# Attention output stage: one semaphore per kind of result, the first product two turns ahead of its norm, and the first norm's scale and shift applied in ScalarE's copy

## The reference, cut to what matters

```python
out = outs.transpose(1, 0, 3, 2, 4).reshape(Bb, Ll, dm)
out = _ln(out, post_w, post_b, eps=1e-05)      # first norm, scale post_w, shift post_b
return out @ wo                                # y, 256 wide
```

## Time and profile before

| what | value |
|---|---|
| median of 3 runs | 451.33 us (451.16 to 452.99) |
| the profiled execution's own time | 449.57 us |
| its span, first to last instruction | 447.8 us |
| granted TensorE clock, mean over the span | 0.93 of full |
| busy share of the span | PE 86%, DVE 66%, ACT 63%, POOL 39% |
| the changed stage | 239.6 to 308.5 us, 23 turns |

### The profile page before, as it was taken

How to read it: one execution, slowest core, us unless ns; L and a number is a source line. 1 busy time by engine, 2 the same in 40 slices (tenths; PEclk the granted TensorE clock), 3 DMA queues, 4 the chain that set the end, 5 groups by cost and what they waited for, 6 DMA issues and landing times. The chain is left out here.

```text
span 447.8 us, 11346 instructions
## 1 busy us (share of the span) xinstructions
PE 384.3 (86%) x3744; PEld 262.3 (59%) x3744; DVE 293.7 (66%) x1029; ACT 281.6 (63%) x710; POOL 173.4 (39%) x298
## 2 busy tenths in 40 slices
PE   1999998959999999999982999975698587799993
PEld 1544343438777787778761667762443164577883
DVE  4757529355777777777773487864869975455185
ACT  4778676554766766776663566653679992551634
POOL 1405728023888888888875013233000000000003
PEclk9999999987999999999996799985979977899997
DMA  8221233251122222222235300000000000000003
GB/s 236 34 84 37 73 103 93 86 176 37 51 54 67 70 63 57 68 70 57 61 117 154 72 1 0 2 0 1 0 1 1 0 18 10 1 2 3 4 1 94
DMA packets 33008, 23.07 MB, mean 52 GB/s; under 512 B 10046, under 2 KB 32716, under 8 KB 32972
## 3 DMA queue, kind: packets, MB, share of 16 engines
q1 hardware_dynamic: 31724, 22.54, 18.4%
q10 hardware_dynamic: 1248, 0.07, 0.2%
HBM read 13.13 MB, written 9.47 MB: 50 GB/s over the span
## 5 line engine op out<-in xcount | busy, mean ns | idle before, releaser
L1466 POOL TENSOR_TENSOR win<-win,lng 128x512 f32<-128x512 f32 x2 | 2.5, 1273 | 125.5 <-ACT win L1745 125.5
L967 ACT ACTIVATE win<-bank 128x384 f32<-128x384 f32 (+1 forms) x124 | 44.2, 412 | 9.7 <-PE bank L910 9.1
L479 PE MATMUL bank<-w,hT 128*128 128x385 f32 x128 | 45.4, 495 | 0.4 <-ACT stage L605 0.4
L888 PE MATMUL bank<-win,wst 128*32 128x128 f32 x1024 | 44.2, 283 | 1.3 <-ACT kd L962 1.3
L479 PEld LDWEIGHTS bank<-w,hT 128*128 128x128 f32 x128 | 23.2, 189 | 24.5 <-issue 11.4
L888 PEld LDWEIGHTS bank<-win,wst 128*32 128x32 f32 x1024 | 26.6, 110 | 9.2 <-ACT kd L962 1.5
L1239 ACT ACTIVATE std_<-mv_,cst 128x2 f32<-128x2 f32 (+1 forms) x46 | 13.5, 296 | 28.5 <-DVE mv_ L1217 14.5
L1189 POOL TENSOR_TENSOR xn<-xn,out_b 128x128 f32<-128x128 f32 x16 | 7.3, 455 | 50.9 <-ACT xn1T L1255 50.9
L1034 POOL TENSOR_SCALAR xh<-raw,bmv,brs 128x128 f32<-128x128 f32 x32 | 25.5, 797 | 2.6 <-DVE brs L1086 2.5
L877 PE MATMUL bank<-win,cst 128*128 128x128 f32 x128 | 25.1, 278 | 0.9 <-ACT raw L988 0.9
L1027 POOL TENSOR_TENSOR xkm<-win,wst 128x256 f32<-128x256 f32 x32 | 19.7, 615 | 12.5 <-PE bank L926 6.0
(11 more groups left out here) (300 smaller groups left out, 1117.3 us busy)
## 6 DMA issues: line engine op xcount, KB each, us to landing
rows_scratch<-stage SPq DMA_DIRECT2D x32, 192.5 KB
win<-rows_scratch SPq DMA_DIRECT2D x32, 192.5 KB, 2.4
attn_scratch<-ob SPq DMA_DIRECT2D x32, 64.0 KB
att<-attn_scratch SPq DMA_DIRECT2D x4, 512.0 KB, 4.1
xt<-in_L_attn_x SPq DMA_DIRECT2D x4, 256.0 KB, 4.3
out<-win SPq DMA_DIRECT2D x4, 256.0 KB, 2.4
cst<-in_constants SPq DMA_DIRECT2D x1, 408.0 KB, 5.2
w<-in_L_attn_wk SPq DMA_DIRECT2D x2, 128.0 KB, 4.3
```

The lines of the kernel that those rows point to most:

```text
L479: mm = nc.tensor.matmul(rows_bank(i, h)[:, 0:RC], hT[:, k, i * P:(i + 1) * P], w4[:, k, h, :], start=(k == 0), stop=(k == 1))
L888: mm = nc.tensor.matmul(dst[32 * b:32 * b + 32, 0:F], v[:, at:at + 2 * K], w_sb[:, state, first_slot(b) + h, :], start=False, stop=(h == 1 ...
L967: nc.scalar.activation(w_sb[:, state, at:at + n, :], bank[b][:, 0:n * F].rearrange("f (h g) -> f h g", h=n), ACT.Copy).then_inc(w_done, 1)
```

## The change

The stage keeps its arithmetic but for the first norm. It now runs as follows.

- Each kind of result has a semaphore of its own: `yn_done`, `y2_done`, `y_mm`, `h_mm`, `h_read`, `norm_done`, `x_mm`, `x_done`. `mm_done` and `act_norms` are gone; DVE no longer waits at a turn's start for PE's previous turn.
- y is made in turn 2 and its norm is taken in turn 4 instead of 3 (three banks hold y in rotation), and the steps behind it move with it: transposes of y2 in turn 5, h in 6, its statistics in 7, xn1 in 8, the transposes of xn1 in 9. There are 25 turns.
- One `std` and one reciprocal serve all three norms of a turn. xn1 of a tile is written one turn later than its statistics.
- On PE the transposes of yn and of y2 come first, then h, then y, then the transposes of xn1, which now wait for DVE and ACT at a turn's end and not at its start.
- `wo` is loaded as it is. ACT's copy of the transposed yn becomes two pieces of 128 columns, each with its own scale and shift per partition (`post`), instead of one plain copy of 256 columns. The one-row bias product is gone, and in `layer0_in` the products L551, DVE's copy L420 and DVE's two scalings L424.

The core of the difference; of the lines taken out of the three programs of `layer0_out`, which stand in full in the functions above, the plus lines are the replacement:

```diff
-        wo_bias = take(7 * HD, HD, 1)
+        post = take(7 * HD, 4).rearrange("p (n k) -> p n k", n=2)
...
-                    dve.wait_ge(bias_mm, 2)
-                    ch.mark(nc.vector.tensor_copy(wo_bias, bank[5][0:1, 0:HD]))
...
-                        ch.mark(nc.vector.tensor_scalar(wo[:, k, :], wo_raw[:, k, :], post_w[:, k:k + 1], None, ALU.mult))
...
-                        mm = nc.tensor.matmul(bank[5][0:1, 0:HD], post_b[:, k:k + 1], wo_raw[:, k, :],
-                                              start=(k == 0), stop=(k == 1))
-                    mm.then_inc(bias_mm, 1)
...
+        A_TR, Y_PROD, Y_STAT, H_TR, H_PROD, H_STAT, X_OUT, X_TR = 1, 2, 4, 5, 6, 7, 8, 9
+        TURNS = NT + X_TR
+        NORMS = NT + H_STAT
+        TURN_W = NT + Y_STAT
+        LAST_CP = TURN_W + 1
...
+        y_bank = lambda n: bank[(2, 3, 7)[n % 3]][:, 0:HD]
+        h_bank = lambda n: bank[4 + n % 2][:, 0:D]
+        x_bank = bank[6][:, 0:P]
...
+                for n in range(NORMS + 1):
                     p = n % 2
+                    ks = []
+                    if on(n, 0):
+                        if n % B == 0:
+                            dve.wait_ge(at_in[n // B], 16)
+                        mark(nc.vector.bn_stats(st[:, 0, :], at[:, tile(n), :]))
+                        ks.append(0)
+                    if on(n, Y_STAT):
+                        dve.wait_ge(y_mm, n - Y_STAT + 1)
+                        mark(nc.vector.bn_stats(st[:, 1, :], y_bank(n - Y_STAT)))
+                        ks.append(1)
+                    if on(n, H_STAT):
+                        i = tile(n - H_STAT)
+                        dve.wait_ge(h_mm, n - H_STAT + 1)
+                        nc.vector.tensor_tensor(xt[:, i, :], xt[:, i, :], h_bank(n - H_STAT), ALU.add).then_inc(h_read, 1)
+                        dve.wait_ge(h_read, n - H_STAT + 1)
+                        mark(nc.vector.bn_stats(st[:, 2, :], xt[:, i, :]))
+                        ks.append(2)
+                    if ks:
+                        dve.wait_ge(stats, marks[0])
                         for k in ks:
                             ins = nc.vector.bn_aggr(mv[:, p, k, :], st[:, k, :])
                         ins.then_inc(var_done, 1)
+                    if on(n, X_OUT):
+                        i = tile(n - X_OUT)
+                        dve.wait_ge(rs_done, 2 * n)
+                        nc.vector.tensor_scalar(xn1[:, i, :], xt[:, i, :], mv[:, 1 - p, 2, 0:1], rs[:, 1 - p, 2:3],
                                                 ALU.subtract, ALU.mult).then_inc(norm_done, 1)
+                    if ks:
+                        dve.wait_ge(std_done, n + 1)
+                        nc.vector.reciprocal(rs[:, p, :], std[:, p, :]).then_inc(rs_done, 1)
+                        dve.wait_ge(rs_done, 2 * n + 1)
+                        nc.vector.scalar_tensor_tensor(out=shift[:, p, :], in0=mv[:, p, 0:2, 0], scalar=-1.0, in1=rs[:, p, 0:2],
+                                                       op0=ALU.mult, op1=ALU.mult).then_inc(rs_done, 1)
...
+                    if n < NORMS:
+                        act.wait_ge(var_done, n + 1)
+                        nc.scalar.activation(std[:, p, :], mv[:, p, :, 1], ACT.Sqrt, bias=con("eps5")).then_inc(std_done, 1)
+                    if 0 < n <= LAST_CP:
                         act.wait_ge(tr_mm, n)
+                        if on(n, A_TR):
+                            for k in range(2):
+                                ins = nc.scalar.activation(tT[:, p, 0, k * P:(k + 1) * P], bank[p][:, k * P:(k + 1) * P],
+                                                           ACT.Identity, bias=post[:, 1, k:k + 1], scale=post[:, 0, k:k + 1])
+                        if on(n, H_TR):
                             ins = nc.scalar.activation(tT[:, p, 1, :], bank[p][:, HD:2 * HD], ACT.Copy)
                         ins.then_inc(cp_done, 1)
+                    if on(n, 0) or on(n, Y_STAT):
+                        act.wait_ge(rs_done, 2 * n + 2)
                     if on(n, 0):
                         nc.scalar.activation(yn[:, p, :], at[:, tile(n), :], ACT.Identity, bias=shift[:, p, 0:1],
+                                             scale=rs[:, p, 0:1]).then_inc(yn_done, 1)
+                    if on(n, Y_STAT):
+                        nc.scalar.activation(y2[:, p, :], y_bank(n - Y_STAT), ACT.Identity, bias=shift[:, p, 1:2],
+                                             scale=rs[:, p, 1:2]).then_inc(y2_done, 1)
+                    if on(n, X_TR):
+                        i = tile(n - X_TR)
+                        act.wait_ge(x_mm, n - X_TR + 1)
+                        nc.scalar.activation(xn1T[:, i * P:(i + 1) * P], x_bank, ACT.Copy).then_inc(x_done, 1)
...
+                    if 3 <= n <= LAST_CP:
                         pe.wait_ge(cp_done, n - 2)
+                    if on(n, A_TR):
+                        pe.wait_ge(yn_done, n)
                         for k in range(2):
                             ins = nc.tensor.transpose(bank[p][:, k * P:(k + 1) * P], yn[:, 1 - p, k * P:(k + 1) * P], con("ident"))
+                    if on(n, H_TR):
+                        pe.wait_ge(y2_done, n - H_TR + 1)
                         for k in range(2):
                             ins = nc.tensor.transpose(bank[p][:, HD + k * P:HD + (k + 1) * P], y2[:, 1 - p, k * P:(k + 1) * P], con("ident"))
+                    if n <= LAST_CP:
+                        ins.then_inc(tr_mm, 1)
+                    if on(n, H_PROD):
+                        i = tile(n - H_PROD)
                         pe.wait_ge(cp_done, n - 1)
+                        if n - H_PROD >= 2:
+                            pe.wait_ge(h_read, n - H_PROD - 1)
+                        dst = h_bank(n - H_PROD)
                         nc.tensor.matmul(dst, ffnT[:, i * P:(i + 1) * P], con("ident"), start=True, stop=False)
                         for k in range(2):
                             ins = nc.tensor.matmul(dst, tT[:, 1 - p, 1, k * P:(k + 1) * P], up[:, k, :], start=False, stop=(k == 1))
+                        ins.then_inc(h_mm, 1)
+                    if on(n, Y_PROD):
+                        pe.wait_ge(cp_done, n - 1)
+                        for k in range(2):
+                            ins = nc.tensor.matmul(y_bank(n - Y_PROD), tT[:, 1 - p, 0, k * P:(k + 1) * P], wo[:, k, :],
+                                                   start=(k == 0), stop=(k == 1))
+                        ins.then_inc(y_mm, 1)
+                    if on(n, X_TR):
+                        pe.wait_ge(norm_done, n - X_TR + 1)
+                        wait(pe, x_done, n - X_TR)
+                        nc.tensor.transpose(x_bank, xn1[:, tile(n - X_TR), :], con("ident")).then_inc(x_mm, 1)
```

More of the change, by code:

```diff
@@ L1185, in _ @@
                 pool.wait_ge(m1.w_in, 16 * m1.loads)
-                for n in range(7, TURNS):
-                    i = tile(n - 7)
-                    pool.wait_ge(cp_done, n)
+                for n in range(NT):
+                    i = tile(n)
+                    pool.wait_ge(x_done, n + 1)
                     nc.gpsimd.tensor_tensor(xn1[:, i, :], xn1[:, i, :], m1.out_b[:], ALU.add)
@@ L1216, in _ @@
                         for k in ks:
                             ins = nc.vector.bn_aggr(mv[:, p, k, :], st[:, k, :])
-                        if not ks:
-                            ins = nc.vector.memset(mv[:, p, 2 * part, :], 1.0)
                         ins.then_inc(var_done, 1)
-                    dve.wait_ge(std_done, 2 * n + 1)
-                    nc.vector.reciprocal(rs[:, p, 0:2], std[:, p, 0:2]).then_inc(rs_done, 1)
-                    dve.wait_ge(rs_done, 3 * n + 1)
-                    nc.vector.scalar_tensor_tensor(out=shift[:, p, :], in0=mv[:, p, 0:2, 0], scalar=-1.0, in1=rs[:, p, 0:2],
-                                                   op0=ALU.mult, op1=ALU.mult).then_inc(rs_done, 1)
@@ L1253, in _ @@
[L1253 to L1255 removed]
+                            ins = nc.scalar.activation(m1.w_outT[:].rearrange("p k d -> p (k d)"), bank[3][:, HD:2 * HD], ACT.Copy)
                         ins.then_inc(cp_done, 1)
[L1257 to L1259 removed]
+                    if on(n, 0) or on(n, Y_STAT):
+                        act.wait_ge(rs_done, 2 * n + 2)
```

103 lines of the change are left out of this document (20 added, 83 removed).

## The result

| | before | after |
|---|---|---|
| median of the runs, us | 452.16 (451.16 to 453.87, 4 runs) | 427.73 (424.98 to 431.72, 4 runs) |
| profiled execution, us | 449.57 | 425.5 |
| its span | 447.8 | 423.7 |
| stage (first memset of `mv` to layer 1) | 239.70 to 308.53 = 68.83 | 238.12 to 292.02 = 53.90 |
| layer 1 (same code in both) | 139.3 | 131.7 |

The ratio is 0.944, 95% interval 0.935 to 0.952: faster. Ratios and intervals leave out executions more than 1.5% above the fastest of the same kernel (one of e14's among them, 539.70 us at a mean clock of 0.643); in the batches of e5 to e12 and of e17 and e18 these are most of before's, which puts the ratio there about 0.01 above the quotient of the medians. The direction was right; the size was not. Forecast were 439.9 and a range of 436 to 445.5, a gain of 11.4; the measured gain is 24.4, and 24.1 in the span of the two profiles.

The account below looks back on a forecast made before the run. PE's own work and a two-turn ring were taken to bound the stage at 3.17 us a turn. At 2.6 a turn the stage saves 10.4 and the input stage 1.0, 11.4 together: median 439.9 us, range 436 to 445.5.

Parts of the forecast that it names:

- The ring of 2.55: Stage's middle: ACT's copies, yn, y2 and PE's transposes of y2 form a one-turn ring of 2.55 us.
- rings at 2.41: Stage's middle: DVE's own ring at 2.41 us and PE's work at 2.41 to 2.65 interlock with ACT's ring.
- What bounds the kernel now: Stage before the change: PE's 3.03 us a turn and a two-turn ring of 3.15 to 3.2 each both bound.
- Start: Stage's first turns at clock 0.50: PE bounds at 2.56 us a turn; turn 5 starts at 251.6.
- End: Stage's end from turn 20: before's 8.80 us at clock 0.50 plus 1.0 for the longer pipeline.
- rival 2: Larger gain: turn of 2.55 us and PE at full clock to the stage's end; 437.1 us, chance 0.12.
- The four turns without a new tile: Stage's turns 16 to 20: DVE's ring is 2.07 us without first statistics, 8.2 us in all.
- The rest of the kernel "moves as a whole": Scan and layer 1, untouched, start when the stage before ends and keep their length; no gain counted.
- Input stage: Removing L551's bias products, which held PE's queue 1.02 us, saves 1.0 us, bounds 0 and 1.0.
- Rival 1: ScalarE takes over as the stage's bound at 3.0 us a turn; 444.3 us, chance 0.20.
- Rivals 3: PE's clock falls in the stage as it waits for y2; turn about 4.8 us, up to 464 us, chance 0.03.
- 4 (the turn doesn't shorten): An overlooked order of waits holds the stage's turn at 3.2 to 3.5 us; 446.5 to 450 us, chance 0.07.

Follow-up runs that it names:

- e14: The changed kernel with eight memsets on DVE at the stage's start, so the stage comes 5.3 us later; median 436.02 us, ratio 0.967 to before.
- e5: The kernel before with five extra 128x512 products in each of layer 1's TensorE waits for gated rows; median 456.35 us, ratio 1.023 to before.
- e12: The changed kernel with a separate semaphore for yn's transposes and y2's transposes moved to bank 6; median 432.58 us, ratio 0.967 to before.
- e17: The changed kernel again, unchanged, timed with before in five rounds; median 432.02 us against before's 451.67.
- e18: e13 again, unchanged, on the same chip as e17; median 430.6 us, ratio 0.968 to before.
- e4: The changed kernel with one plain 256-column copy for the two scaled pieces, leaving out the first norm's scale and shift; 425.49 us, ratio 0.942 to before.
- e2: The changed kernel with before's plain copy, bias row and input stage, so the pipeline change alone; median 444.89 us, ratio 0.985 to before.
- e1: The kernel before with only the split copy, folded wo and no bias row or input-stage bias product; median 445.57 us, ratio 0.987 to before.
- e6: The changed kernel with five extra products in each of layer 1's TensorE waits for gated rows; median 435.6 us, ratio 0.977 to before.
- e16: The kernel before, unchanged, run once more for a second profile; 452.77 us in one run.
- e8: The kernel before with eight memsets on DVE at the stage's start, delaying it 5.3 us; median 457.53 us, ratio 1.023 to before.
- e9: e1 with one square root and reciprocal a turn for all three norms, xn1's steps a turn later; median 441.33 us, ratio 0.988 to before.
- e15: The changed kernel with four memsets on DVE at the stage's start, delaying it 2.6 us; median 435.92 us, ratio 0.967 to before.
- e13: e12 with x's transpose straight behind y2's and its copy ahead of yn; median 429.67 us, ratio 0.954 to before.
- e7: e6 with nine small 128x128 products added at the stage's start; median 435.3 us, ratio 0.976 to before.

## Why the prediction was wrong in size

**The ring of 2.55 and the turn.** Right, and by its terms: pieces at a step of 0.35, copies 0.70 and 0.26, yn 0.50, y2 0.57, transposes 0.44. e4 shows that it was the bound. The forecast of 2.6 allowed for an interlock with rings at 2.41; they are at 2.27 or less (e4), and PE's work alone at 2.28 (e2). That was 0.5 us over eleven turns. The bias row's 0.62 and the waits at nothing were right.

**What bounds the kernel now.** Incomplete: PE's 3.03 and the ring over two turns stood there, the ring over one turn through the second square root did not (e1). It changed no term, since the change removes that as well, but whoever had forecast the affine part alone from my section would have promised a gain in the turn and got a loss.

**Start.** "From there PE bounds: 2.56", with turns 3, 4, 5 at 6.8, 9.4 and 11.9 after the stage's start. They came at 6.43, 8.54 and 10.43. The term was mis-sized: two rows of PE that follow each other overlap, 242.36 to 242.84 for the transposes and 1.71 for the products, 2.19 where I had added 0.69 and 1.87. In e6, at a clock of 0.50 for the whole 10.4 us, turn 5 came at 10.69; so the overlap is 1.2 of the 1.5 us and the clock that rose before turn 5 the other 0.3.

**End.** "8.80 at clock 0.50; I add 1.0." It took 7.28 at 0.88, 2.5 us less than the 9.8 of the sum. Part of it is the clock: in before's own code the stretch from the first weight transposes to the stage's end took 8.66 at 0.50, 8.09 at 0.63 (e16) and 7.54 at 0.85 (e8), so up to 1.1. The other 1.4 is the code, and here the step "I add 1.0" failed: after's code takes 7.26 to 7.28 from its last transposes of y2 to the end in each of six profiles, at clocks of 0.87 to 1.00. The last tiles' xn1 follow each other closely, since a turn there has one square root and not two. The last transposes of xn1, first of before, then of after:

```profile
303.98 0.42 PE L1291 MATMUL bank<-cst,xn 128*128 128x128 f32 x1
306.54 0.45 PE L1291 MATMUL bank<-cst,xn 128*128 128x128 f32 x1 [2.14 <-DVE xn L1230]
```

```profile
289.26 0.30 PE L1315 MATMUL bank<-cst,xn 128*128 128x128 f32 x1 [0.64 <-ACT xn1T L1270]
290.02 0.30 PE L1315 MATMUL bank<-cst,xn 128*128 128x128 f32 x1 [0.46 <-ACT xn1T L1270]
```

e9, before's order with one square root, has 7.61 from the last transposes of y2 to the end where e1 has 10.19, at clocks of 0.83 and 0.65. My rival 2 had the turn of 2.55 and a shorter end, at a chance of 0.12, but it put the end down to the clock alone.

**The four turns without a new tile.** 8.2 forecast, 8.10 measured.

**The rest of the kernel "moves as a whole".** This step failed, and it was the largest: 7.6 us where the sum had nothing. Layer 1 has the same code in fifteen of the profiles and took 131.1 to 139.3, with DVE busy 90.3 to 90.4 and ACT 82.0 to 82.3 in all of them; PE's busy time went from 105.5 to 113.1 and the mean clock from 0.93 to 0.87. Three profiles of before's code (before, e8, e16) have 138.4 in the mean, four of after's (after, e17, e14, e15) have 134.7. So of the 7.6 some 3.6 hold in the mean, on few profiles, and the rest was which pair of executions was compared. Since all have the same 1160 records of PE in layer 1, the places can be found by counting. Up to the 101st record before's code takes 39.5 to 39.9 and after's 37.4 to 37.5, in every one of these seven profiles: 2.2 that hold. From the 141st to the 261st it is 30.5 to 31.1 in six of the seven and 26.0 in after's first profile alone (and in e1 and e13): 4.7 of the 7.6 that were luck. In that stretch lie these rows, of before, of after and of e17, after's second profile:

```profile
374.95 2.09 PE L1497 MATMUL bank<-ffnT,cst 2*128 2x512 f32 x8 [2.73 <-DVE he L1785]
```

```profile
355.94 1.14 PE L1502 MATMUL bank<-ffnT,cst 2*128 2x512 f32 x8 [2.68 <-DVE he L1790]
```

```profile
357.23 2.09 PE L1502 MATMUL bank<-ffnT,cst 2*128 2x512 f32 x8 [2.71 <-DVE he L1790]
```

The Trainium skill ("TensorE: Matmul & The Clock Gate", Part 1) has it that idling brings the throttle back; the rows agree as far as that the falls come behind TensorE's waits (e5), but one wait of 2.73 in before was followed by a fall and one of 2.68 at the same place in after was not, while in e16 one of 2.68 was.

**Input stage.** Right in direction; its size can't be told well. The pair shows 0.54 at the scan's start; over all profiles, six with before's input stage start the scan at 98.97 in the mean (97.76 to 100.03) and fourteen with the other's at 97.40 (96.75 to 98.16): 1.6, for a forecast and upper bound of 1.0, with a spread of 2.3 among the six. The scan itself, unchanged, is another 0.9 shorter in the mean of the fourteen, for a forecast of 0 and with no cause shown. PE's row where L551 stood:

```profile
29.05 0.50 PE L548 MATMUL bank<-ln_b,up_raw 128*128 128x1 f32 x4
```

**In sum.** Four profiles of before's stage (68.83, 68.81, 72.39, 71.41) and four of after's (53.90, 54.20, 53.89, 54.02) differ by 16.4 in the mean, against a forecast of 10.4. After's stage is the steadier one as well: its turn 5 begins 10.4 to 10.7 after the stage's start (delays taken off), whatever the clock, while before's turn 6 begins at 17.5 or at 20.5. With 2.5 ahead of the stage and 3.6 in layer 1 that makes 22.5, between the two measured differences of medians, 24.4 and 19.65. Even the lower one is outside the forecast range: 432 against 436.

**Rivals.** Rival 1 (ScalarE bounds at 3.0): ScalarE's ring bounds, but at 2.55. Rivals 3 (the clock falls) and 4 (the turn doesn't shorten) did not come. Rival 2 was the nearest, at 437.1, and still 9 above the measured median.

**Left open.** What decides whether the clock falls behind a given wait in layer 1. Its length changes between executions of one program (e16, e17), so the changes in e14 and e15 can't be put down to the moment of entry; the experiments with extra products didn't hold it. Nor is the mean clock the whole of it: e4's layer 1 has the highest, 0.93, and took 133.6, e13's has 0.92 and took 131.1. Why the head of layer 1 is 2.2 shorter behind after's stage is open too.

## What to carry to other kernels

List every ring, over one turn and over two, with its length, before costing a part of a change: where three bounds lie at 3.0 to 3.2, taking away one gives little, and a part that costs on its own (e1, a longer turn) can be what lets the others pay. Don't assume that code behind the change moves as a whole: compare the busy times of its engines and the granted clock, and take a second profile of before, since one execution's clock enters a forecast as if it were a property of the code. Cost the last turns of a pipeline on their own: with fewer steps in them a turn is shorter, and more turns need not take more time. A wait on TensorE that fits into other work is free (e2), but filling it with dummy products only helps if nothing behind it waits longer for coming sooner; here it gave 0.4 us at most (e7).
